# A fused four-layer transformer block: half of the second layer's value projection moved between stages, and the experts' output biases added by VectorE

## The reference

```
# layer 0
x = x + tanh(g0) * inter_token_attention(layernorm(x), ctx)   # 8 groups x 8 heads x 16 keys, head size 2
x = x + tanh(g4) * moe(layernorm(x))    # 8 experts, top 2, capacity 256: gelu(x @ W1[e] + b1[e]) @ W2[e] + b2[e]
# layer 1: 16 heads of 64
value = einsum('btd,dnh->bnth', ctx, w_value)     # ctx (8*512 x 128) @ w_value (128 x 1024)
x = x + tanh(g1) * attention(layernorm(x), ctx -> key, value)
# then an int8 product, layer 2 (attention, 16 experts), layer 3 (attention, ternary product)
```

## Time and profile before

| | us |
|---|---|
| median of 3 runs (lowest, highest) | 1560.88 (1560.24, 1569.34) |
| the profiled execution, its own time | 1564.25 |
| its span | 1562.5 |
| TensorE busy | 1375.8 |
| VectorE busy | 1051.3 |
| ScalarE busy | 796.8 |
| GpSimd busy | 628.8 |

### The profile page before, as it was taken

The page is one execution under the profiler, slowest core; times in us unless marked ns, Lnnn a source line. Parts: engine busy times, 40 slices in busy tenths (PEclk is TensorE's granted clock), DMA queues, the critical chain, the costliest instruction groups (busy, mean ns, idle before and its releaser), DMA issues. The chain is left out here.

```text
span 1562.5 us, 29870 instructions
## 1 busy us (share of the span) xinstructions
PE 1375.8 (88%) x10324; PEld 739.4 (47%) x10332; DVE 1051.3 (67%) x3269; ACT 796.8 (51%) x1144; POOL 628.8 (40%) x446
## 2 busy tenths in 40 slices
PE   5999878559999999999538999998999759999995
PEld 4444355525666666666413333333677513333332
DVE  4988743266676666765578777773566788777756
ACT  3777723336565566654243555555443206555553
POOL 4767513415676667668332211210400182222200
PEclk9999978858999999999667999999899959999997
DMA  4555645435442344310243333510400022422200
GB/s 149 207 210 222 231 152 162 141 121 216 149 156 63 128 149 155 118 46 2 33 106 74 88 70 71 112 28 2 99 2 1 8 48 43 66 47 40 40 6 27
DMA packets 88921, 147.89 MB, mean 95 GB/s; under 512 B 16769, under 2 KB 61980, under 8 KB 85191
## 3 DMA queue, kind: packets, MB, share of 16 engines
q1 hardware_dynamic: 84288, 116.69, 26.3%
q10 hardware_dynamic: 2688, 25.56, 4.2%
q0 software_dynamic: 1808, 3.83, 1.2%
HBM read 93.66 MB, written 45.11 MB: 89 GB/s over the span
## 5 line engine op out<-in xcount | busy, mean ns | idle before, releaser
L1965 DVE CUSTOM_DVE_ANT_0 a_junk<-a_psM,a_madd 128x512 bf16<-128x512 f32 x512 | 332.0, 683 | 90.5 <-issue 87.7
L1908 ACT ACTIVATE a_probs<-a_psE 128x1024 f32<-128x1024 f32 x256 | 262.2, 1024 | 207.2 <-PE a_psE L1784 206.3
L2372 DVE TENSOR_REDUCE a_mx<-a_psM 128x1 f32<-128x512 f32 x236 | 148.2, 669 | 124.1 <-PE a_psM L2196 124.1
L1784 PE MATMUL a_psE<-a_maddT,res_identb 64*128 64x512 bf16 x1024 | 221.5, 386 | 2.1
L1759 PE MATMUL a_psM<-narrow_k_op,narrow_q_op 57*128 57x512 bf16 (+1 forms) x512 | 153.2, 413 | 30.2 <-DVE a_mx L1965 21.1
L2333 ACT ACTIVATE a_probs<-a_psE 128x1024 f32<-128x1024 f32 x128 | 130.9, 1025 | 85.5 <-PE a_psE L2218 82.2
L1795 PE MATMUL a_psO<-a_probs,narrow_values 128*32 128x256 f32 x2048 | 163.2, 392 | 2.6 <-ACT a_probs L1908 1.1
L2166 POOL TENSOR_TENSOR a_half_sum<-a_probs 128x1024 f32<-128x1024 f32 x64 | 150.8, 2356 | 32.4 <-ACT a_probs L2333 32.4
L2214 PE MATMUL a_psE<-a_qT,a_kT 64*128 64x256 f32 x1024 | 133.7, 381 | 0.0
L2230 PE MATMUL a_psO<-a_probs,a_values 128*64 128x256 f32 x1024 | 124.6, 385 | 0.8 <-ACT a_o_raw L2317 0.8
L2354 DVE RECIPROCAL a_o_raw<-a_o_raw 128x256 f32<-128x256 f32 x64 | 111.4, 1741 | 11.0 <-ACT a_o_raw L2317 11.0
(11 more groups left out here) (378 smaller groups left out, 2480.5 us busy)
## 6 DMA issues: line engine op xcount, KB each, us to landing
wide_k<-a_k_stage SPq DMA_DIRECT2D x32, 512.0 KB, 2.6
a_k_part<-wide_k SPq DMA_DIRECT2D x64, 256.0 KB, 3.1
wide_v<-a_v_stage SPq DMA_DIRECT2D x24, 512.0 KB
a_kT<-wide_k ACTq DMA_DIRECT2D x6, 2048.0 KB
a_values<-wide_v ACTq DMA_DIRECT2D x6, 2048.0 KB, 8.7
keys<-a_parts SPq DMA_DIRECT2D x96, 64.0 KB, 1.9
narrow_k_op<-keys SPq DMA_DIRECT2D x30, 192.0 KB
narrow_q_op<-a_y_parts SPq DMA_DIRECT2D x180, 32.0 KB
```

Of the source, the lines that this page charges most:

```text
L1784: return pe.matmul(psE[s % 2][:, j, :, :], res.identb[group, :], maddT[r][group, s % 2 * 2:s % 2 * 2 + 2, :], start=False, stop=last, skip ...
L1908: act.activation(probs[:, head:head + 2, k:k + 2, :], psE[s % 2][:], ACT.Exp).then_inc(exped, 1)
L1965: dve.tensor_tensor_reduce(junk[j][:], psM[j][:], madd[r][:, t, :], 1.0, -3.0e38, ALU.add, ALU.max, mx[r][:, max_place(h, t):max_place(h, ...
L2372: dve.tensor_reduce(mx[r][:, at:at + 1], max_bank(2 * p + t, j, first), AX.X, ALU.max).then_inc(max_read, 1)
```

## The change

- Stage a0a projects only two value tiles of each chunk (KT - LATE_TILES = 2, so n_wide = 12).
- The third tile (k = 2) of all 8 chunks is projected in stage f0e by a new class `SpreadValues`: chunk e beside expert e, one half (a matmul of 128x512 into a bank of its own) behind the expert's hidden layer and the other behind its output. ScalarE copies both out after the expert's four gelus, and SyncE stores the tile from a ring of four buffers.
- psH has three banks instead of four. The weights have four buffers instead of two; SyncE loads experts 2 and 3 right after the late tiles' stores and expert e + 4 when y of expert e is copied.
- b2 is broadcast to 128 partitions by its DMA (64 KB in place of 0.5 KB); the two memsets of b2 and the two bias matmuls per expert go; VectorE adds b2 in the instruction that takes y out of PSUM, behind a new wait for the weights.
- After the last expert's copies ScalarE takes one square root of a single column, for no result of its own.

```diff
+LATE_TILES = 2
 ...
-        n_wide = W_PAIRS + (KT - 1) * VC
+        n_wide = W_PAIRS + (KT - LATE_TILES) * VC
 ...
-                    for k in range(2, KT - 1):
+                    for k in range(2, KT - LATE_TILES):
                         wide_values(i, k, first)
 ...
+class SpreadValues:
+    RING = 4
 ...
+    def tensor(self, pe, n, c):
+        keys = self.res.ctxT[:, 2 * n:2 * n + 2].rearrange("d t n c -> d (t n c)")[:, self.k * P:(self.k + 1) * P]
+        if VC * n + c >= 1:
+            pe.wait_ge(self.out, VC * n + c)
+        pe.matmul(self.bank[:], keys, self.res.w1v[:, c * CHUNK:(c + 1) * CHUNK], start=True, stop=True).then_inc(self.made, 1)
+    def scalar(self, act, n, c):
+        act.wait_ge(self.made, VC * n + c + 1)
+        if c == 0 and n >= self.RING:
+            act.wait_ge(self.stored[n % self.RING], 16 * (n // self.RING))
+        act.copy(self.stage[n % self.RING][:, c * CHUNK:(c + 1) * CHUNK], self.bank[:]).then_inc(self.out, 1)
+    def sync(self, sp, n):
+        sp.wait_ge(self.out, VC * (n + 1))
+        sp.dma_start(self.res.wide_v[n, :, self.k], self.stage[n % self.RING][:]).then_inc(self.stored[n % self.RING], 16)
 ...
-    AHEAD = 4
+    AHEAD, WEIGHTS, H_BANKS = 4, 4, 3
 ...
-                    sp.dma_start(b2[b][0:1, :], io["L0_b2"][e:e + 1]).then_inc(w_in[b], 16)
-
-                sp.wait_ge(zeroed, 2)
+                    sp.dma_start(b2[b][:], io["L0_b2"][e].partition_broadcast(P)).then_inc(w_in[b], 16)
 ...
-                for e in range(2, E):
-                    sp.wait_ge(made, e - 1)
-                    load(e, e % 2)
+                for e in range(2, WEIGHTS):
+                    load(e, e)
+                for e in range(E):
+                    spread.sync(sp, e)
+                    if e + WEIGHTS < E:
+                        sp.wait_ge(y_copied, e + 1)
+                        load(e + WEIGHTS, e % WEIGHTS)
                 late.finish(sp)
+                spread.finish(sp)
 ...
-                        if e > 0:
-                            pe.wait_ge(acted, (e - 1) * HC + k + 1)
+                        n = e * HC + k
+                        if n >= H_BANKS:
+                            pe.wait_ge(acted, n - H_BANKS + 1)
 ...
+                    spread.tensor(pe, e, 0)
 ...
-                        pe.matmul(psY[b][:, r, :], res.ones[:], b2[b][:], start=True, stop=False)
 ...
                     last.then_inc(made, 1)
+                    spread.tensor(pe, e, 1)
 ...
+                    for c in range(VC):
+                        spread.scalar(act, e, c)
+                act.activation(res.root[:], res.ones[:, 0:1], ACT.Sqrt)
 ...
-                for b in range(2):
-                    dve.memset(b2[b][:], 0.0).then_inc(zeroed, 1)
 ...
-                    dve.tensor_copy(y[:, e], psY[e % 2]).then_inc(y_copied, 1)
+                    dve.wait_ge(w_in[e % WEIGHTS], 64 * (e // WEIGHTS + 1))
+                    dve.tensor_tensor(y[:, e], psY[e % 2], b2[e % WEIGHTS][:].unsqueeze(1).to_broadcast([P, ROW_HALVES, D]), ALU.add).then_inc(y_copied, 1)
```

More of the change, by code:

```diff
@@ L273, in attend_layer0 @@
     k_stage = [outer.sb(f"k_stage{i}", [P, 2, S2]) for i in range(4)]
-    v_stage = [outer.sb(f"v_stage{i}", [P, WIDE_V]) for i in range(KT - 1)]
+    v_stage = [outer.sb(f"v_stage{i}", [P, WIDE_V]) for i in range(KT - LATE_TILES)]
     parts = [outer.sb(f"parts{i}", [P, 3, CHUNK], BF16) for i in range(2)]
@@ L307, in attend_layer0 @@
         wide_made, wide_out = ph.sem("wide_made"), ph.sem("wide_out")
-        wk_stored, wv_stored = [ph.sem(f"wk_stored{i}") for i in range(4)], [ph.sem(f"wv_stored{i}") for i in range(KT - 1)]
+        wk_stored, wv_stored = [ph.sem(f"wk_stored{i}") for i in range(4)], [ph.sem(f"wv_stored{i}") for i in range(KT - LATE_TILES)]
         minus_done = ph.sem("minus_done")
@@ L390, in _ @@
                                              parts[l][j * GROUP_ROWS:(j + 1) * GROUP_ROWS, part, :]).then_inc(k_stored[l], 16)
-                    for k in range(KT - 1):
+                    for k in range(KT - LATE_TILES):
                         sp.wait_ge(wide_out, n_wide * n + W_PAIRS + VC * (k + 1))
@@ L821, in finish, with __init__ @@
         sp.wait_ge(self.stored, 16 * len(self.chunks))
+class SpreadValues:
+    RING = 4
+    def __init__(self, ph, res, k, bank):
+        self.res, self.k, self.bank = res, k, bank
+        self.stage = [ph.sb(f"spread{j}", [P, WIDE_V]) for j in range(self.RING)]
+        self.made, self.out = ph.sem("spread_made"), ph.sem("spread_out")
+        self.stored = [ph.sem(f"spread_stored{j}") for j in range(self.RING)]
+    def tensor(self, pe, n, c):
[11 more added lines that the diff above has]
+        sp.dma_start(self.res.wide_v[n, :, self.k], self.stage[n % self.RING][:]).then_inc(self.stored[n % self.RING], 16)
+    def finish(self, sp):
+        for j in range(self.RING):
+            sp.wait_ge(self.stored[j], 16 * B // self.RING)
 def layer0_experts(nc, io, res):
@@ L1002, in queued_experts @@
     C = L0_CAPACITY
-    AHEAD = 4
+    AHEAD, WEIGHTS, H_BANKS = 4, 4, 3
     with Phase(nc, "f0e") as ph:
[L1005 to L1008, removed]
+        w1 = [ph.sb(f"w1_{i}", [P, H]) for i in range(WEIGHTS)]
+        w2 = [ph.sb(f"w2_{i}", [P, HC, D]) for i in range(WEIGHTS)]
+        b1 = [ph.sb(f"b1_{i}", [P, HC]) for i in range(WEIGHTS)]
+        b2 = [ph.sb(f"b2_{i}", [P, D]) for i in range(WEIGHTS)]
         xg = ph.sb("xg", [P, E, ROW_HALVES, D])
@@ L1101, in _ @@
                     b = e % 2
-                    act.wait_ge(w_in[b], 64 * (e // 2 + 1))
+                    act.wait_ge(w_in[e % WEIGHTS], 64 * (e // WEIGHTS + 1))
                     if e >= 2:
```

17 lines of the change are left out of this document (10 added, 7 removed).

## The result

The changed kernel runs in 1574.1 us (median of 12 runs, 1566.9 to 1579.8), the kernel before, measured beside it, in 1561.5 us (12 runs, 1560.0 to 1570.2). The ratio is 1.0065, with a 95% interval from 1.005 to 1.008. I had forecast 1561.3 us in a range of 1555 to 1567: wrong by 12.8 us, and outside of the range. The profiled execution took 1573.61 us with a span of 1571.8, against 1564.25 and 1562.5 before: 9.3 us more span, some 3 us less than the difference of the medians.

What follows compares the result with a forecast made beforehand. The prediction took a0a as bound by its exponentials (TensorE's pace, then GpSimd's chain) and f0e by TensorE while rows are there. Terms summed to +0.4 us on 1560.9, giving 1561.3 us, range 1555 to 1567.

Steps and rivals of the forecast that it cites:

- A period of 19.48 us in a0a, six times 0.95: Stage a0a: each pair of exponentials shortens by 0.95 us from 20.43, for pairs 1 to 6: -5.7 us.
- The split of the legs: Stage a0a: exponentials 11.0 and 8.5 us apart; only the first leg shortens, GpSimd's chain holds the second.
- rival 1: Stage a0a: TensorE's whole time comes back, up to 12.0 us; taken as 1557 us, chance 0.17.
- The end of the stage, -1.1: End of a0a: one value store fewer saves 0.57 us, the bias row landing sooner 0.5; -1.1 us together.
- Experts, +7.7: Stage f0e: half tiles stretch the period from 4.18 to 5.6 us, expert 0 adds 0.7; last y +7.7 us.
- Rival 2: Stage f0e, transposes of experts 4 to 7: experts wait for gathered rows behind the stores; 1566 us, chance 0.2.
- Load back, +0.3: After the last y: the load back also waits for the last tile's store; +0.3 us, from 0 to +1.3.
- Square root, -0.8: Norm after the experts: square root's table load moves into ScalarE's wait for the load back; -0.8 us.
- The sum, +0.4: Whole kernel: -5.7 - 1.1 + 7.7 + 0.3 - 0.8 = +0.4 us; the experts take back what attention gives.

Runs made afterwards that it cites:

- the two with the move undone: Changed kernel plus SyncE's wait for unit 0's rows, third value tile made in a0a again, no half tiles beside the experts: 1571.0 us (0.9986) and 1571.7 us (0.9996).
- kernel before with the wait: Kernel before, with SyncE waiting until unit 0's query rows have landed before issuing unit 1's masks, keys and positions: 1570.9 us, ratio 0.9994.

## Why the prediction was wrong, by its own steps

- **A period of 19.48 us in a0a, six times 0.95: right.** 19.47 measured; the last exponential moved by 5.7 us against the first odd one. The split of the legs (11.0 and 8.5, GpSimd's chain holding the second) was right too, so rival 1, 12.0 us of TensorE's time back, was out.
- **The end of the stage, -1.1:** the value stores fell from 1.70 to 0.95 us, but the twelve key stores took 8.09 us instead of 7.67, so SyncE gave 0.3 net for my 0.57. The wait for the bias row fell from 2.91 to 1.93 us, 1.0 for my 0.5. From the last exponential to the experts' first transpose the changed kernel saved 2.0 us; the kernel before's own second profile differs from its first by 2.9 in the same stretch, so this term can't be told more closely.
- **Experts, +7.7:** 6.7. y0 came 0.64 us later behind the first transpose (I had 0.7), the pitch was 5.50 for my 5.6, the seven steps 38.27 for my 39.2. Between them row waits were gone, as assumed, in all four profiles of the changed experts' stage without halts; two of these have a wait of 0.5 and 0.7 us before the first expert. Rival 2 was out.
- **Load back, +0.3:** 0.45. **Square root, -0.8:** 1.0 (the stretch from the last y to layer 1's first query matmul fell by 0.55, in spite of 0.45 for the load back).
- **The sum, +0.4:** the terms as measured add up to -0.9 (-5.7, -1.3, +6.7, +0.45, -1.0). The traces as a whole have -1.6 in the first pair of profiles up to layer 1's first query matmul, +1.2 in the pair of the second chip, both after taking off where stage a0a's first odd exponential stood (3.1 us later in one profile). The forecast lies between them.
- **The step that failed** is the last and unwritten one: that everything behind norm n2 only shifts. The sum was carried to the end of the kernel with no term for the 1235 us behind it. The runs put a term of 8.4 us (paired, third chip) to 11.0 us (second chip) there, for the queue race at the start of layer 2's attention. In the profile of before it could be seen that this place was close: the first maximum waited 7.29 us for rows issued by two engines, and 512 KB loads were issued 0.33 us before the last of them was out. My range had 6 us upwards for terms in the touched stages only.

What makes the change late for this race every time is told only in part. The clock's rise came 3.0 to 3.6 us behind the first query matmul in all five profiles of kernels with the old stages, and 4.8 to 5.9 in all ten with the new ones; the two with the move undone had 6.0 and 3.0. Why it falls so was not settled, and no run set it by hand. Nor is the rest of the difference of the result's medians (12.6 us, of which the race is 8 to 11 and the touched stages about 0) traced run by run; the ten profiles with the new stages also need 0.7 to 6.1 us more from the first maximum to the end than the 748.9 us of the kernel before, and clock drops of a few microseconds fall at other places in them.

## What to carry to other kernels

A change that moves time by a few microseconds re-draws every close race behind it. So read, in the profile of before, not only the touched stages but each stage's first wait for small transfers with bulk queued right behind them, and put a term and a width for it into the forecast. In the code, don't let an engine issue the next unit's bulk until the current unit's rows have landed, or issue both from one queue in the order of need: in the kernel before it cost nothing (0.9994), in the changed one it was worth 8 us and more. And compare two versions on more than one chip before a verdict of half a per cent: 1.0071 and 1.0025 are the same two kernels.

## What the runs showed of the hardware that I had not expected

- Order beats load. With the last two or three of 12 small transfers issued behind 1 MB of masks, and keys in packets of 8 KB after it, the matmul that needs all twelve came 8 to 12 us later, though the small ones came from another engine's queue. With the same bytes in another order it came at +12.65 to +14.81.
- SyncE's six issues take 4.84 to 4.86 us in three profiles with ScalarE's issues 0.5 us behind them, and 4.02 or 4.03 in eight with ScalarE's 1.0 to 1.5 us behind. It is not simply how close the two engines start, since with both in the same instant they took 4.06, and at 0.23, 0.34, 1.6 and 2.65 us they took 4.64, 4.07, 4.50 and 4.43. 0.8 us of this is half of what decided who was first; what makes it stays open.
- On two of three chips VectorE and ScalarE halt in the experts' stage, at the same two places in every profile (eleven of eleven; the two with the move undone have a third long step), 4.3 to 5.3 us in all for the kernel before; the six other profiles have none. With the half tiles in TensorE's queue 1.3 to 1.4 us of it is left. In the trace TensorE's semaphore counts of a whole expert arrive together at the end of a halt (kernel before with the wait: four hidden matmuls that began over 1.9 us from 274.05 on count at 276.05, 276.09, 276.14 and 276.18). What holds them was not tried and stays open.
